# A conv/attention chain on one Trainium2 core: values, maxima and sums of a narrow step issued one unit later

## The reference, cut to what matters

```python
weight = jnp.einsum('bct,bcs->bts', q * scale, k * scale)      # 8 heads of 32 channels, 1024 x 1024
weight = jax.nn.softmax(weight.astype(jnp.float32), axis=-1)
h = jnp.einsum('bts,bcs->bct', weight, v)
h = jnp.einsum('oc,bct->bot', proj_w, h) + proj_b[None, :, None]
return (xf + h).reshape(b, c, *spatial)
```

## Time and profile before

| | |
|---|---|
| time, three runs | 5362.62 us median (5360.14 to 5363.67) |
| the profiled execution, its own time | 5362.61 us |
| its span, first to last instruction | 5360.8 us |
| PE busy | 4897.9 us (91%) |
| POOL busy | 3268.5 us (61%) |
| DVE busy | 2833.4 us (53%) |
| ACT busy | 2577.3 us (48%) |
| mean granted TensorE clock | 0.948 of full |

### The profile page before, as it was taken

The page is one execution under the profiler, slowest core; times in us unless marked ns, Lnnn a source line. Parts: engine busy times, 40 slices in busy tenths (PEclk is TensorE's granted clock), DMA queues, the critical chain, the costliest instruction groups (busy, mean ns, idle before and its releaser), DMA issues. The chain is left out here.

```text
span 5360.8 us, 63346 instructions
## 1 busy us (share of the span) xinstructions
PE 4897.9 (91%) x22016; PEld 2258.4 (42%) x22016; DVE 2833.4 (53%) x5112; ACT 2577.3 (48%) x4641; POOL 3268.5 (61%) x1969
## 2 busy tenths in 40 slices
PE   7788899998999989999899989999899998999887
PEld 3235333543335433354334543345334453345434
DVE  5354566255662566535664366644566345662362
ACT  3353565435563456624555246552556525554252
POOL 4473677546674567735777357763677636776363
PEclk8799999999899999999999999999999999999898
DMA  3111211021210221102210122201122012120010
GB/s 86 29 31 51 52 46 41 20 54 45 50 35 20 60 54 39 36 22 66 51 46 20 35 53 56 48 13 45 43 56 54 7 50 56 42 50 11 19 45 12
DMA packets 103608, 221.20 MB, mean 41 GB/s; under 512 B 31104, under 2 KB 33408, under 8 KB 103168
## 3 DMA queue, kind: packets, MB, share of 16 engines
q1 hardware_dynamic: 103296, 217.16, 15.7%
HBM read 56.47 MB, written 8.39 MB: 12 GB/s over the span
## 5 line engine op out<-in xcount | busy, mean ns | idle before, releaser
L962 DVE TENSOR_REDUCE max_cols<-bank 128x1 f32<-128x512 f32 x3456 | 2182.5, 680 | 1742.1 <-PE bank L517 1736.9
L852 ACT ACTIVATE probs<-bank 128x512 f32<-128x512 f32 x3456 | 1931.5, 600 | 2332.9 <-PE bank L517 2130.4
L1179 POOL TENSOR_TENSOR probs_added<-probs_added,probs 128x1024 f32<-128x1024 f32 x768 | 1799.8, 2374 | 61.9 <-ACT probs L852 61.7
L517 PE MATMUL bank<-q_stack,k_stack 97*128 97x512 f32 (+1 forms) x3584 | 1655.1, 518 | 82.9 <-DVE max_cols L962 35.5
L517 PE MATMUL bank<-probs,v_tokens 128*32 128x512 f32 (+1 forms) x7168 | 1374.3, 634 | 49.9 <-ACT probs L852 49.9
L517 PEld LDWEIGHTS bank<-q_stack,k_stack 97*128 97x128 f32 (+1 forms) x3584 | 657.9, 194 | 768.8 <-issue 383.6
L517 PE MATMUL bank<-act,weight_stream 128*128 128x512 f32 x1792 | 926.0, 617 | 24.4 <-ACT probs L852 6.9
L1179 POOL TENSOR_TENSOR probs_added<-probs 128x1024 f32<-128x1024 f32 x192 | 453.7, 2368 | 681.0 <-ACT probs L852 670.8
L1166 POOL TENSOR_TENSOR probs_added<-probs 128x512 f32<-128x512 f32 x48 | 61.1, 1273 | 757.6 <-PE bank L517 725.2
L517 PEld LDWEIGHTS bank<-probs,v_tokens 128*32 128x32 f32 (+1 forms) x7168 | 322.4, 122 | 475.2 <-issue 315.2
L517 PE MATMUL bank<-high_parts 32*128 32x512 f32 x3072 | 402.6, 512 | 130.9 <-DVE max_cols L962 96.5
(11 more groups left out here) (85 smaller groups left out, 3336.1 us busy)
## 6 DMA issues: line engine op xcount, KB each, us to landing
k_stack<-high_parts SPq DMA_DIRECT2D x384, 128.0 KB, 2.4
q_stack<-high_parts SPq DMA_DIRECT2D x768, 64.0 KB, 2.0
weight_stream<-stream_dram SPq DMA_DIRECT2D x32, 768.0 KB, 4.3
k_stack<-low_parts SPq DMA_DIRECT2D x192, 128.0 KB, 2.4
q_stack<-low_parts SPq DMA_DIRECT2D x384, 64.0 KB, 2.0
act<-x_dram SPq DMA_DIRECT2D x8, 1024.0 KB, 6.5
act<-pos_dram SPq DMA_DIRECT2D x8, 1024.0 KB, 5.8
weight_stream<-stream_dram SPq DMA_DIRECT2D x16, 512.0 KB, 3.7
```

The source lines that it names most:

```text
L517: return nc.tensor.matmul(dst, lhsT, rhs, start=start, stop=stop, **kw)
L852: act.activation(PR[:, m % P_RING, j, :], bank[:, :], ACT.Exp, scale=att.scale).then_inc(reading(key), 1)
L962: dve.tensor_reduce(cols[:, kh, j, qt:qt + 1], bank[:, :], AX.X, ALU.max).then_inc(reading(key), 1)
L1179: pool.tensor_tensor(ADD[:, js, :], one, two, ALU.add).then_inc(p_added, 1)
```

## The change

The three things that stand in `rest` of a narrow attention move by one unit: the values from unit 4i + 6 to 4i + 7 (behind the fourth score of the next item), the quads and their maxima by one (`first_quad`), and the sums with DVE's four pieces from units 34, 35, 36, 36, 37 to 35, 36, 37, 37, 38. `TAIL`, the count of units in which the attention before still has something to do, grows by one. Scores, exponentials, POOL's adds, `columns_at`, all DMAs, the wide attentions, and the table `stages` with its own quads stay where they are. No instruction is added or taken away.

```diff
-TAIL = 13
+TAIL = 14
...
 def first_quad(s):
-    return 32 * (s - 1) - 4 * EARLY_QUADS + 2
+    return 32 * (s - 1) - 4 * EARLY_QUADS + 3
...
 def after_step(att, u, what):
-    off = ((13, 14, 14, 15, 16) if att.wide else (34, 35, 36, 36, 37))[what]
+    off = ((13, 14, 14, 15, 16) if att.wide else (35, 36, 37, 37, 38))[what]
...
 def items_at(att, u):
-    return [(s, i) for s in range(att.steps) for i in range(8) if u == att.per * s + 4 * i + 6]
+    return [(s, i) for s in range(att.steps) for i in range(8) if u == att.per * s + 4 * i + 7]
```

## The result

The changed kernel takes 5382.6 us (median of 12 runs, 5371.14 to 5419.47) against 5362.8 for the kernel before (12 runs, 5349.11 to 5368.75): a ratio of 1.0046, 95% interval 1.0028 to 1.0065. It is 0.46% slower, +20 us. That lies in my range, but the likeliest case, no measurable change, did not come; the slower side did. My range was 52 us wide, and two parts of my sum were wrong in size or at zero, so that the time lies in it says little for the sum.

A forecast was written before the change was run, and what follows sets the result against it. PE's queue was taken to bound most of the span, POOL's adds second. From 5362.61 us, -9 + 8 + 4 - 3 + 0 = 0 gave 5363 us, with an 8-in-10 range of 5338 to 5390.

The forecast's parts named there:

- What bounds the kernel: Whole span: PE's queue sets the time over most of it, busy 4897.9 of 5360.8 us; POOL's adds a second bound.
- Term 1: Ahead of values: waits for the item's fourth exponential go, -9 us, all in the middle stretch; ends 0 and -49.9.
- Term 2: Values and quads torn apart by a score: 42 pairs on balance at 0.15 to 0.2 us each, +8 us.
- Term 3: Changes of step: sums wait for a bank the new step's first score has filled, +4 us; ends 0 and +8.
- Term 4: Changes of step: POOL restarts one score earlier after the added sums, ten times 0.3 us, -3 us.
- The cover of the maxima: Row of maxima at each step: DVE still finishes in time, no cost; without that cover 27 us over 96 steps.
- Term 5: Inserted work keeping its units while values and quads move: no sign of its own, 0 and +-19 us.
- The chain with the norms: DVE statistics and group norm waiting for POOL: one POOL add more or less, 2.36 us, 19 us in eight samples.
- My last line: If time grows by over 20 us, look for new waits behind DVE's maxima in stretches with norms or projections.
- rival "inserted work": Each of eight samples has one POOL add more in a norm chain: +19, so 5382 us; chance 0.18.
- The faster rival: All 19.6 us of middle-stretch waits go and POOL restarts earlier at some twenty changes of step: 5342 us; chance 0.27.
- the argument against it: The quad behind the values takes banks of the same burst of scores, so its wait replaces the values' wait.

The follow-up runs named there:

- before_quads_behind: The kernel before, with only the eight table quads beside block 2's attention one unit later (values, score, quad): 5355.26 us, ratio 0.9992.
- quads_and_maxima_late: The kernel before, with only quads and maxima one unit later in all narrow attentions, values and sums unmoved: 5443.53 us, ratio 1.0152.
- the two rejoined kernels: The changed kernel with block 2's eight table quads one unit later; the second also with the three early quads one unit later: 5366.96 and 5380.01 us.

## Why the prediction was right and wrong

- **What bounds the kernel**: right. By the page, PE's busy time is the same in both kernels, and the difference is idle time of the array. The 8 us of busy time that I wanted to see for torn pairs can't be read off, since the shorter time at half clock pulls the other way.
- **Term 1** (-9, ends 0 and -49.9): the size came, partly by luck. The array's idle time ahead of values fell by 19.1 us (behind ACT from 49.9 to 23.2, not to near 0): 9.0 us in the middle stretch of the earlier trace rows and 10.1 at the ends. But the middle's 9.0 are not the waits that I had counted. The 10.2 us of step 2 of block 1, which I had taken out as POOL's, all went, and the step got no shorter (+0.1 us), so leaving them out of the time was right. The other steps of the middle attentions lost 3.5 us of such waits, and step 3 of block 2 took on 3.8 us of new ones.
- **Term 2** (+8): the step that failed. My price of 0.15 to 0.2 us was read from the earlier trace rows, where the order is values, score, quad, and for that order it is right: 0.14 us in `before_quads_behind`, 0.19 in `quads_and_maxima_late` with its clock and 0.13 without (an estimate). I then netted 70 pairs torn beside block 2 against 28 joined beside block 0 as if all had this price. But the 70 are torn the other way round, quad first. There the quad needs a bank that an exponential still holds, and a pair costs from 0.3 us (step 3 between the two rejoined kernels, 0.9 us for 3 pairs) to 0.66, in kernels that the clock does not blur there. In step 3 of block 2, where all seven pairs are torn, the array's idle time ahead of quads went from 7.2 to 25.6 us over the seven attentions. With the 0.4 measured on the changed kernel: 70 x 0.4 - 28 x 0.14 = +24 us. I had counted the switch of matmul kinds (an idle gap of fixed length) and not asked what the four banks wait for. The fixed gaps themselves are as in the earlier trace rows.
- **Term 3** (+4, ends 0 and +8): right. The array idles 6.4 us ahead of the sums, all at the ends of the program and all behind ACT. At the place of the earlier trace rows the sums' load now starts at 332.19, with the first new exponential starting at 331.54.
- **Term 4** (-3): not to be seen apart. POOL's idle time at the place of the earlier trace rows is 5.64 us instead of 5.84.
- **The cover of the maxima** held: nothing behind `columns_at` got later. The 22.4 us behind `neg_max_t` (L974) in the groups after is the old wait of the earlier trace rows under a new name; with the shift the quad's bank there is that of the turned maxima, and its wait is 3.33 instead of 4.36 us.
- **Term 5** (0, +-19): right as an open risk, wrong in its place and in its sign. The chain with the norms that I named got no POOL add more; both its waits are shorter than in the earlier trace rows, and that turn's block 0 is 3.9 us shorter. What met the shift badly is the projection, in 14 attentions at 1.8 to 1.9 us: +26 us. My last line had named the place to look, behind DVE in the stretches with projections.
- Put together with measured sizes: -19 + 24 + 6 + 26 = +37, against +19 between the spans. A lower share of half clock gives back about 13 us of that, 30 us less of it at 0.44 each (3.0 us for a stretch of 6.8); this is an estimate. The fit to 5 us is no proof: the sum mixes idle time with times of steps, its 19 us hold 10.2 that shortened no step, and it leaves out the 1.0 and 2.3 us by which steps 0 and 1 of each of block 0's attentions got shorter.
- **Rivals**: 5382 us had been the time of the rival "inserted work", and it came out, by another mechanism and together with term 2. The faster rival did not come: of the 19.6 us of the middle stretch 9.0 went, and the idle time ahead of quads grew by more than that, as the argument against it said.

## What to carry to other kernels

When a step of a hand-made order moves, list for each moved instruction which buffers it needs and who frees them last at the new place, and price both orders of a torn pair apart: an instruction that needs several banks costs little behind the work that it stood with and much ahead of it. Work that keeps its place while its surroundings move (here a projection and a table of quads) must move along or be looked at as a new meeting. And a long block of matmuls whose results nobody can use yet should not stand directly ahead of one that feeds the other engines; here that swap is worth 0.6% by the medians and 0.45% at equal clock, though not every change of step gains.

## What the hardware showed that I had not expected

- TensorE's granted clock falls to half for stretches of mostly 3.4 to 27 us, 50 to 84 times in a span, at the same units in nearly all turns of one kernel, and at other units after an edit elsewhere. The rows at 2001.64 and 2002.40 show one that begins 0.8 us after the array idled 1.56 us; what starts the others is open.
- It costs as much as the edits that are tried: one stretch less of 6.8 us made step 0 of block 1 2.8 to 3.1 us shorter in three kernels that did not touch it, and between runs of one kernel 0.001 of mean clock goes with 3.7 us. A difference of 10 us between two kernels of this size says nothing about an edit until the clocks are compared.
- A pair of values and quad torn apart, with the idle weight loads of 0.84 and 0.24 us at its switches, costs 0.11 to 0.19 us of time when the values come first.
